# Other orders in the prologue and the last batch, a later exchange of one slice's low-rank columns, and no multiplications of zeros in the prologue

## The reference

```
x  = x + tanh(g_xattn) * einsum('mk,nk->mn', fp8_round(layernorm(x)), fp8_round(ctx))
h  = layernorm(x)
fused = h @ (Wa * col_scale)        # Q_std, K_std (16 heads x 24), V (512), Q_low, K_low (16 x 8)
q_tail, k_tail = where(w_rec > 0.1, (K_low, Q_low), (Q_low, K_low))   # per head
scores = concat(Q_std, q_tail) . concat(K_std, k_tail) / sqrt(32), causal
x  = x + tanh(g_ffn) * (softmax(scores) @ V) @ Wp
```

## Time and profile before

| what | value |
| --- | --- |
| median of 3 runs | 501.77 us (500.73 to 505.46) |
| the profiled execution | 500.87 us |
| its span | 499.1 us, granted clock 0.978 on average |
| busy: PE, DVE, ACT, POOL | 89%, 67%, 52%, 31% of the span |
| the L876 matmuls (zeros) | 48, the first at 17.8 us, the last at 49.1 us |

### The profile page before, as it was taken

How to read it: one execution, slowest core, us unless ns; L and a number is a source line. 1 busy time by engine, 2 the same in 40 slices (tenths; PEclk the granted TensorE clock), 3 DMA queues, 4 the chain that set the end, 5 groups by cost and what they waited for, 6 DMA issues and landing times.

```text
span 499.1 us, 8044 instructions
## 1 busy us (share of the span) xinstructions
PE 443.6 (89%) x2600; PEld 317.4 (64%) x2600; DVE 333.3 (67%) x1093; ACT 257.2 (52%) x510; POOL 156.5 (31%) x282
## 2 busy tenths in 40 slices
PE   0468799998869999999769999999879999999996
PEld 0244577775536788776535788777545778676765
DVE  3899536879993254788997243788997236566733
ACT  1777446567445570558445463448655424363530
POOL 4988775343223300243213400144122100111110
PEclk9989999999979999999988999999998999999999
DMA  6412083324400345324410234514300144234112
GB/s 215 175 33 85 14 260 91 90 71 107 133 1 2 81 105 153 101 53 98 115 61 2 53 95 98 177 39 105 92 23 1 45 104 102 56 94 102 53 44 85
DMA packets 28217, 42.62 MB, mean 85 GB/s; under 512 B 8304, under 2 KB 8688, under 8 KB 28176
## 3 DMA queue, kind: packets, MB, share of 16 engines
q1 hardware_dynamic: 26752, 41.19, 29.7%
q10 hardware_dynamic: 1232, 0.54, 0.5%
q0 software_dynamic: 192, 0.39, 0.3%
HBM read 12.59 MB, written 4.19 MB: 34 GB/s over the span
## 4 chain that ended last, share of the span: by engine, by line
PE 69%; DVE 16%; POOL 5%; ACT 3%; issue 3%; DMA 2%; SPq 0%; POOLq 0%; DVEq 0%; ACTq 0%
PE pv_bank L788 14%; PE mm_bank L613 9%; PE mm_bank L614 8%; PE mm_bank L615 8%; DVE x_all L1261 6%; PE max_bank L757 6%; PE exp_bank L774 6%; DVE max_bank L1293 3%; PE mm_bank L815 2%; PE mm_bank L817 2%; PE mm_bank L816 2%; PE turn_bank L629 2%; PE pv_bank L797 2%; ACT work L1036 2%; DMA ctx_raw<-in_ctx 2%
## 5 line engine op out<-in xcount | busy, mean ns | idle before, releaser
L1293 DVE CUSTOM_DVE_ANT_0 max_bank<-max_bank,causal 128x512 f32<-128x512 f32 (+3 forms) x256 | 121.6, 509 | 58.1 <-PE max_bank L757 49.8
L1036 ACT ACTIVATE work<-exp_bank 128x512 f32<-128x512 f32 (+1 forms) x192 | 94.6, 528 | 89.9 <-PE exp_bank L774 88.8
L527 POOL TENSOR_SCALAR_AFFINE_SELECT work<-work 128x384 f32<-128x384 f32 x64 | 33.5, 524 | 280.6 <-ACT work L1036 280.6
L788 PE MATMUL pv_bank<-work,v_aug 128*33 128x256 f32 (+3 forms) x512 | 78.5, 449 | 0.8 <-POOL work L530 0.8
L757 PE MATMUL max_bank<-k_stack,q_stack 96*128 96x512 f32 x248 | 67.8, 338 | 5.4 <-DVE row_max L1293 5.4
L774 PE MATMUL exp_bank<-q_stack,k_stack 97*128 97x512 f32 (+3 forms) x256 | 69.1, 335 | 3.5 <-ACT work L1036 1.8
L1261 DVE SCALAR_TENSOR_TENSOR x_all<-mm_bank,coef,x_all 128x128 f32<-128x128 f32 x224 | 61.1, 341 | 0.2 <-issue 0.2
L788 PEld LDWEIGHTS pv_bank<-work,v_aug 128*33 128x33 f32 x512 | 28.4, 113 | 49.4 <-issue 40.0
L613 PE MATMUL mm_bank<-xt_hi,w_hi 128*128 128x512 f32 x128 | 54.1, 422 | 1.5 <-POOL w_lo L543 1.5
L774 PEld LDWEIGHTS exp_bank<-q_stack,k_stack 97*128 97x128 f32 x256 | 45.5, 189 | 14.9 <-ACT work L1036 4.8
L1276 DVE SCALAR_TENSOR_TENSOR qk_lo<-mm_bank,col_root,qk_hi 128x512 fp32r<-128x512 f32 x32 | 24.0, 748 | 44.8 <-ACT qk_hi L1007 44.8
(11 more groups left out here) (176 smaller groups left out, 810.8 us busy)
## 6 DMA issues: line engine op xcount, KB each, us to landing
q_stack<-qk_hi SPq DMA_DIRECT2D x128, 64.0 KB, 2.0
k_stack<-qk_hi SPq DMA_DIRECT2D x120, 64.0 KB, 2.0
ctx_raw<-in_ctx SPq DMA_DIRECT2D x16, 256.0 KB, 3.3
x_all<-in_x SPq DMA_DIRECT2D x16, 256.0 KB, 4.6
q_stack<-qk_lo SPq DMA_DIRECT2D x64, 64.0 KB, 2.0
out<-x_all SPq DMA_DIRECT2D x16, 256.0 KB, 2.5
k_stack<-qk_lo SPq DMA_DIRECT2D x60, 64.0 KB, 2.0
work<-in_L_ffn_Wa SPq DMA_DIRECT2D x3, 768.0 KB, 9.4
```

What stands on the lines that cost most here:

```text
L527: pool.affine_select(out=three, in_=three, compare_op=ALU.is_ge, fill=0.0, base=0, pattern=[[0, 3], [1, P]], channel_multiplier=-1)
L788: last = pe.matmul(pv_bank[64 * j:64 * j + D + 1, P * m:T], v_aug[:, m, 2 * u + j, :], prob[j][:, PROB_COL[m]:PROB_COL[m] + T - P * m], st ...
L1036: act.activation(prob[j][:, UNIT_COL[k]:UNIT_COL[k] + UNIT_LEN[k]], exp_bank[(3 * j + k) % 2][:, 0:UNIT_LEN[k]], ACT.Exp, scale=SCALE).the ...
L1293: last = dve.tensor_tensor_reduce(max_bank[unit % 2][:, col:col + width], max_bank[unit % 2][:, col:col + width], causal[:, T - width:T], ...
```

## The change

It rewrites the orders of the prologue and of the last batch on TensorE, ScalarE, VectorE and POOL, and takes out the twelve `w` groups of zeros. The pieces of work are otherwise the same. `T3` moves on VectorE from ahead of S0 to behind S10 and b1; its companion `b3` on ScalarE to ahead of N1. `l0` on POOL moves behind s2 and s3. `c`, `D` and `p` change places behind q0. In the last batch, K2.0, Q3, K3 and the Y pieces move to other places among the maxima and exponentials.

```diff
 PE_LAST = [
-    "v3.0 rowmax max0 max1 Q2.01 max2 v3.1 max3 exp0 exp1 max4 Q2.2 exp2 v3.2 max5 exp3 v3.3 Q2.3 exp4 exp5",
...
-    "K3.1 rowmax K3.2 max0 max1 pv exp0 max2 max3 exp1 K3.3 exp2 z0 exp3 max4 max5 exp4 Y0 exp5 back",
...
-    "max0 Y4 rowmax max1 pv max2 max3 exp0 exp1 Y5 exp2 max4 max5 back exp3 exp4 Y6 exp5",
+    "v3.0 rowmax max0 Q2.0 max1 Q2.1 v3.1 max2 exp0 Q2.2 max3 exp1 max4 v3.2 exp2 exp3 v3.3 exp4 max5 Q2.3 exp5 K2.0",
...
+    "max0 rowmax K3.23 max1 pv exp0 max2 exp1 Y0 exp2 max3 exp3 back max4 exp4 z0 max5 exp5",
...
+    "Y4 rowmax max0 max1 pv max2 exp0 exp1 max3 Y5 exp2 exp3 max4 back exp4 max5 exp5 Y6",
     "rowmax Z0 pv exp0 exp1 Y7 exp2 exp3 z2 back exp4 exp5 Z1",
 ]
...
-PE_FIRST = ("f0 w0 w1 f1 w2 f2 f3 w3 w4 f4 w5 S0 S1 f5 S2 S3 f6 S4 w6 S5 S6 S7 w7 S8 "
-     "S9 S10 S11 w8 f7 S12 w9 f8 S13 w10 S14 f9 w11 S15 v0 v1.01 f10 v1.2 f11 v1.3 q0.0 B0 q0.123 k0.0 "
-     "B1 k0.123 V2 M0 M1 q1.01 M2 q1.23 k1.01 M3 k1.2 M4 k1.3 M5")
-
-ACT_FIRST = ("d0 C0 a0 a1 C1 C2 C3 b0 C4 C5 f4 b1 C6 f5 s0 a2 f6 s1 C7 e3 b2 f7 a3 N0 "
-     "s2 N1 f8 f9 s3 b3 v0 N2 N3 f10 f11 v1 q0 p0 k0 c0 V2 D0 D1 q1 c1 c2 k1 c3")
-
-DVE_FIRST = ("t0 t1 t2 t3 w0 A0 A1 x0 x1 x2 x3 T0 L0 L1 F0 F1 G0 L2 L3 F2 f0 F3 f1 f2 "
-     "G1 T1 T2 c0 f3 T3 S0 S1 S2 S4 S5 S6 b0 S8 b1 S9 S10 S12 S13 h0 S14 u0 b2 b3 "
-     "h1 u1 u2 u3 h2 h3 B0 B1 q0 k0 M0 M1 M2 M3 q1 M4 M5 k1")
-
-POOL_FIRST = ("s0 s1 i0 l0 s2 s3 s4 s5 s6 s7 j0 l1 j1 a0 l2 a1 r0 r1 l3 a2 j2 a3 r2 r3 "
-     "o0 j3 g0 g1 D0 g2 g3 D1 p0 v0")
+PE_FIRST = ("f0 f1 f2 f3 f4 S0 S1 f5 S2 S3 f6 S4 S5 S6 S7 S8 S9 S10 S11 f7 S12 S13 S14 f8 "
+     "f9 S15 v0 v1.012 f10 f11 v1.3 q0.012 B0 q0.3 k0.0 B1 k0.123 V2 M0 M1 q1 M2 k1.012 M3 M4 k1.3 M5")
+
+ACT_FIRST = ("d0 C0 C1 a0 C2 a1 b0 C3 C4 a2 C5 f4 C6 b1 f5 s0 a3 f6 b2 C7 s1 e3 f7 N0 "
+     "b3 N1 f8 s2 f9 s3 v0 N2 N3 f10 f11 q0 v1 k0 p0 c0 V2 D0 c1 q1 D1 c2 k1 c3")
+
+DVE_FIRST = ("t0 t1 w0 t2 t3 A0 A1 x0 x1 x2 x3 T0 f0 L0 L1 F0 f1 L2 F1 G0 L3 F2 F3 G1 "
+     "f2 T1 f3 c0 T2 S0 S1 S2 S4 S5 S6 S8 S9 b0 S10 b1 T3 S12 S13 u0 h0 S14 h1 b2 "
+     "u1 b3 u2 u3 h2 h3 B0 B1 q0 k0 M0 M1 q1 M2 M3 M4 M5 k1")
+
+POOL_FIRST = ("s0 s1 i0 s2 s3 l0 s4 s5 s6 s7 l1 j0 l2 j1 a0 a1 l3 r0 r1 j2 a2 a3 r2 r3 "
+     "o0 j3 g0 g1 g2 D0 D1 g3 v0 p0")
...
 END_LAST = {
     "PE": "Z2 pv Z3 back Z4 Z5 z3 Z6 Z7 Z8 Z9 Z10 Z11",
     "ACT": "copy z3",
-    "DVE": "Z2 norm Z3 z3 Z8 Z9 Z10 Z11",
+    "DVE": "z2 Z1 Z2 norm Z3 z3 Z8 Z9 Z10 Z11",
 }
...
                 if kind == "f":
                     first_turn(i)
-                elif kind == "w":
-                    for _ in range(4):
-                        pe.matmul(exp_bank[1][:, 0:T - P], causal[:, 0:P], causal[:, 0:T - P], start=True, stop=True)
```

## The result

The kernel after takes 498.73 us (median; 495.99 to 502.89), the kernel before 501.85 on the same chips (497.14 to 505.46): the ratio is 0.9944, 95% interval 0.9923 to 0.9965. That is 2.8 us less (1.8 to 3.9), where I had forecast 0.6 less and a range from 499.3. The two profiles show where work stands, the runs what it is worth.

What follows compares the result with a forecast made beforehand. TensorE was taken to bound the dense stages, and the prologue to count through q0's start. q0 -0.4 and -0.2 behind it made -0.6, taking the median 501.77 to 501.2 us, range 499.3 to 505.0.

Steps and rivals of the forecast that it cites:

- Bound: Whole kernel: TensorE's dense stages can win only idle time; the prologue is worth exactly what it does to q0's start.
- Block sums start sooner, -3.0: VectorE in the prologue: with T3 moved behind S10, the first block sum S0 starts at 33.1, not 36.06: -3.0 us.
- POOL up to s7, 0: POOL in the prologue: a later G0 offsets the 1.73 us wait before s6, so s7 still ends at 32.18: 0.
- rival 4: POOL's 1.73 us before s6 goes as well and the clock rises at once: -2.9, 498.9 us; chance 0.15.
- T3 comes back, 1.6 (3.4 high): VectorE behind S10: T3 costs 1.6 us beside POOL's short steps, 3.4 at the high price; S14 ends at 50.1 or 51.8.
- ScalarE's queue and a3: ScalarE in the prologue: b3 waits for T3, s3 is done at 51.1, POOL's a3 starts -0.6; q0 -0.7, bounds -0.9 and +0.8.
- No zeros, and the clock: TensorE in the prologue: removed zeros give no time as work but lower the clock; between two cases, q0 -0.4 us.
- (b): TensorE: the clock rises in the middle of v0, six matmuls at +0.24; q0 keeps -0.7 us.
- (c): TensorE: the clock rises at v0's end; v1.012 ends at 57.8, h3 at 60.3, q0 +0.4 us.
- From q0 on, -0.2, last batch 0: Behind q0: -0.2 us from tenths of hidden waits in the score section and last batch; last batch 0, bounds -0.3 and +1.5.
- rival 1: TensorE: the low clock lasts through v0 and v1; 505.0 to 510.8 us, middle 507.5; chance 0.09.
- rivals: 2: VectorE: T3 keeps the high price beside POOL, +0.8, with v0 a microsecond later too: 502.9 us; chance 0.20.

Runs made afterwards that it cites:

- b1: Kernel after with POOL's o0 moved behind j3 and TensorE's f10, f11 spread into v1; ratio to the kernel before 0.9959, and again 0.9946.
- x2: Kernel after with VectorE's T3 alone put back between T2 and S0; ratio to the kernel before 1.0009.
- x1: Kernel before with VectorE's T3 alone moved from ahead of S0 to behind S10; ratio to the kernel before 1.0011.
- y2: Kernel after with POOL's l3 alone moved back behind r0, so beside T3; ratio to the kernel before 0.9970.
- c1: Kernel after with seven groups of zeros put back, from S9 to S15, to hold the clock for v0; ratio to the kernel before 0.9951.
- after_again: Kernel after, unchanged, timed and traced once more; ratio to the kernel before 0.9950.
- e2: Kernel before with the four new prologue orders, zeros out, and the old last batch; ratio to the kernel before 0.9943.
- e3: Kernel before with only the new orders of the last batch and epilogue; ratio to the kernel before 1.0001.
- y1: Kernel after with all four engines' prologue orders from q0 on as in the kernel before; ratio to the kernel before 0.9952.
- before again: Kernel before, unchanged, timed and traced once more against itself; ratio 1.0003.
- e4: Kernel after with the twelve groups of zeros put back; ratio to the kernel before 0.9963.
- b2: Kernel after with o0 behind j3, f10 and f11 spread into v1, and seven groups of zeros put back; ratio to the kernel before 0.9924, median 497.25 us.

## Why the prediction was wrong

The chain was the forecast one, but one overlap in it was misjudged and one price was too high, both of them upstream of POOL's a3; and they explain less than half of the miss.

1. *Bound.* Half right. The dense stages did not move. That the prologue is worth exactly what it does to q0 was not shown: from T0, q0 came 1.2 us sooner and the time fell by 2.8, it came 1.1 sooner again in b1 and the time stayed, and in x2 it stood 2.0 later than before with 0.5 us more (-1.0 to 1.9).
2. *Block sums start sooner, -3.0.* S0 at 32.06, from T0 -3.8: 0.8 better.
3. *POOL up to s7, 0.* **This step failed.** I set G0's delay against the 1.73 us before s6. From T0, s7 ended 1.25 us earlier: G0 came only 0.6 us later than before (8.02 for 7.42), not 2, and the idle time that this made was 0.62, while G1 came 1.7 us earlier (11.16 for 12.86) and all of the 1.73 went. It is rival 4's mechanism. The x that the block sums need goes through it, so the better term 2 fits it too: x1, with POOL's old order, has S0 only 2.2 us earlier.
4. *T3 comes back, 1.6 (3.4 high).* **This step was mis-sized.** It took 0.81. I took T1 (1.57) for the price of an exchange that nothing hinders. It was hindered itself, in its middle exchange, which rows 5 left out. Of before, VectorE:

```profile
28.60 1.05 DVE L1326 COPY_PREDICATED x_all<-x_all,work 128x128 f32<-128x128 uint32 x1
```

That ends at 29.65, and POOL's s6, 28.45 + 1.04, at 29.49. The bare price was to be read from the copy and the last exchange alone, 0.28 and 0.29. x2, y2 and the kernel after give 3.93, 1.70 and 0.81, with long POOL operations beside all of T3, beside its copy alone, and beside none of it.

The Trainium skill (SBUF — State Buffer, "SBUF: two separate sides") says that the port pair shared by VectorE and GpSimd is an exclusive lock, held for the whole instruction by the one that has it. The rows of x2 and y2 agree: VectorE's operation, which started second, ends 0.15 us after POOL's, however long POOL's is.
5. *ScalarE's queue and a3.* Forecast S14's end 50.1, T3 at 44.3 to 45.9, s3 done and a3 at 51.1; measured 48.24, 42.99 and 49.76. S14 is 1.86 early, by 1.04 of S0 and 0.8 of T3, and a3 inherits 1.3 of it. Behind a3 the 8.1 us were right: 49.76 + 8.1 = 57.9, the end of w_lo.
6. *No zeros, and the clock.* Right: near (b) in this trace, towards (c) in two others. The clock fell at 44.1, v0's first products took 0.43 and it rose at 50.9, between v0's sixth and seventh of twelve. c1 shows what it cost, 8.85 - 8.07 = 0.8 us of v0 and v1, hidden in this trace since POOL holds q0 to the same moment. In after_again and e2 it was not hidden. There v0 and v1 took 9.47 and 9.54 us, and of after_again these are TensorE's q0, POOL's last w_lo and VectorE's h3:

```profile
58.66 0.50 PE L612 MATMUL mm_bank<-xt_hi,w_hi 128*128 128x512 f32 x1 [0.88 <-DVE xt_lo L1308]
57.28 0.73 POOL L542 TENSOR_TENSOR w_lo<-x_all,w_hi 128x256 fp32r<-128x256 f32 x1
57.93 0.68 DVE L1308 TENSOR_TENSOR xt_lo<-exp_bank,xt_hi 128x512 fp32r<-128x512 f32 x1
```

POOL was done at 58.01, VectorE at 58.61: 0.6 us. Early in the prologue the clock was down too, though the granted clock reads 1.00 there. The turns tell it, in the kernel after:

```profile
31.75 1.50 PE L628 MATMUL exp_bank<-part_sign,v_aug 128*128 128x128 fp8e4 x12
33.95 0.84 PE L628 MATMUL turn_bank<-part_sign,v_aug 128*128 128x128 fp8e4 x12
```

All six turns up to 31.75 take 1.44 to 1.50; before, the second took 0.84.
7. *From q0 on, -0.2, last batch 0.* Last batch right to 0.1 us (e3). Behind q0 nothing came (y1). In rival 1 the middle of 505.0 and 510.8 is 507.9, not 507.5.

So q0, forecast at -0.4, starts 1.7 us earlier from T0 in the two profiles. Over more traces the gap is smaller: 44.47, 43.87 and 43.87 with the old prologue (before, before again, e3), 42.74, 42.86, 43.00 and 43.00 with the new one (after, after again, e2, y1), so 44.07 - 42.90 = 1.2 in the mean (1.6 between those without the wait for `gates`, 0.9 between those with it). That makes 0.8 of the 2.2 us that the forecast missed. The rest stays **open**. The runs show 2.8 us in two independent kernels (after and e2), and single profiles find 1.2 of it before q0 and no fixed place behind: from q0 to the pv of step 7 in the third batch they scatter from 336.3 to 342.3 us in old and new kernels alike. That the new order of the prologue makes the falls of the clock behind q0 rarer or shorter would fit, but the traces, if anything, speak against it. From q0 to that pv the clock was low for 19.3 us in the mean of the six traces with the old prologue (13.7 to 27.3), and for 22.3 in the eleven others (17.1 to 27.3). The timed runs don't show it either: their mean granted clock is 0.972 before and 0.966 and 0.968 after, where the prologue's fall is in it, and 0.974 in e4, which keeps the zeros.

Rival 4's 498.9 lies beside the measured 498.73 partly by luck: its wait before s6 did go, but the clock did not rise at once, and q0 gained 1.2 to 1.7 us of the 2.6 it asked for. The other rivals: 2 did not happen because POOL has only short steps beside T3 (y2 shows the edge of it), 1 ended near case (b), 3 and 6 are refuted by e3 and by q0, and 5, over 1%, did not come.

## What to carry to other kernels

Price a small VectorE copy by what POOL runs at that moment, not by its size: one code put back beside long POOL steps took all of a 0.6% gain (x2), and in the old kernel, moved to a place where POOL had long steps as well, it brought nothing (x1). When one idle time is said to take the place of another, compute both from the rows, since a delay of one input is not the delay of its consumer. Where three engines arrive together, as at q0, relieve them together: with the clock held and POOL as it was (c1) TensorE only waited 1.70 us at q0, and only the rows there say who is next.

## What the runs showed of the hardware

**VectorE's copy ends with POOL's operation.** 0.26 us alone, 1.17 and 1.91 beside subtractions of 512 and 768 columns, ending 0.15 us behind them each time. In this kernel it is seen on COPY and COPY_PREDICATED with both operands in SBUF. Smaller operations show the same: in the kernel after a TENSOR_SCALAR of 128x8 takes 0.17 us at 23.05, with POOL idle, and 0.73 at 25.64, ending at 26.37, where POOL's product ends at 26.34.

**The clock fell where TensorE was busy.** The kernel before, once more, by stage in the first scores:

```profile
68.00:69.00 1.00, 1.00 (x8) 0.92 (x6) 0.68 (x2) 0.49 (x2) 1.00 (x3) 1.00 0.74 168
70.00:71.00 1.00, 1.00 (x4) 0.67 (x2) 0.00 (x0) 0.00 (x0) 0.90 (x3) 0.50 0.88 252
```

TensorE is busy 1.00 of 1.00 us in both, with 8 products in the first and 4 in the second; the granted clock went to 0.50, the level of 1.2 GHz, from 69.3 to 76.2. TensorE's last idle time ahead of the fall was 0.59 us, before 67.24. The same is seen at 78.2 to 81.6 in the kernel after, where the last idle time of 0.3 us or more ended at 69.00, from 77.3 in b2 and from 81.9 in x2. From q0 to the first pv before_again, after, b2 and x2 have 33.94, 31.69, 31.78 and 31.69 us; the others have 30.22 to 30.31. It is one of six traces with the old prologue and three of eleven with the new one, too few to lay it to an order. I have no cause for it. It is some of the scatter that hides effects below 2 us in a single profile.
